# A six-stage decoder megakernel: weights get homes that outlive a stage, and are loaded one stage ahead

## The reference, cut to what matters

```python
x = _layernorm(x + _L0_attn_ref(x, ...))            # state space scan, both directions
x = _layernorm(x + _L0_xattn_ref(ctx_1024, x, ...)) # cross attention, 1500 context rows
x = _layernorm(x + _L0_ffn_ref(x, router_w, w1, w2))  # 8 experts, top 2, squared relu
x = _layernorm(x + _L1_attn_ref(x, ...))            # Mamba block: in_proj, conv, dt, b, c, scan, out_proj
x = _layernorm(x + _L1_xattn_ref(x, ctx_1024, ...)) # causal attention, 16 heads of 8
x = _layernorm(x + _L1_ffn_ref(x, gate_weight, bias, gate_proj, up_proj, down_proj))  # 8 gated experts
```

## Time and profile before

| what | value |
|---|---|
| median of three runs | 1306.85 us |
| the profiled execution, its own time | 1308.4 us |
| its span, first to last instruction | 1306.6 us |
| experts 0, from the stage's first instruction to its last | 728.3 to 807.9 us |
| Mamba: the two loading blocks | 809.1 to 823.7 us |
| Mamba: the scan block | 906.5 to 1115.0 us |
| causal attention, block of the projections | 1134.4 to 1159.3 us |
| experts 1 | 1240.7 to 1306.6 us |

### The profile page before, as it was taken

One profiled execution on the slowest core, in us unless ns is written; L12 is line 12 of the kernel. 1 busy time (PEld: TensorE's weight loads), 2 busy tenths in 40 slices (PEclk: granted clock), 3 DMA queues, 4 the chain that ended last, 5 costly groups with the idle time before them and its releaser, 6 DMA issues. The chain is left out here.

```text
span 1306.6 us, 22904 instructions
## 1 busy us (share of the span) xinstructions
PE 1032.5 (79%) x8295; PEld 737.2 (56%) x8295; DVE 1021.1 (78%) x2092; ACT 699.1 (54%) x1468; POOL 559.6 (43%) x869
## 2 busy tenths in 40 slices
PE   2899887556699999999997793572888888577686
PEld 1555454344699999999996563220333333445555
DVE  4699999666698888899975466549999999567465
ACT  3867554025466666666662442343666666147444
POOL 3100000012888888888853220101777777114351
PEclk9999888768899999999999797665899999879889
DMA  1000000011211111111000100000000000100001
GB/s 42 1 1 2 2 1 1 2 62 47 93 49 72 73 72 72 71 69 69 32 2 1 33 1 19 4 1 0 0 1 1 1 1 1 39 1 3 2 25 29
DMA packets 16850, 32.49 MB, mean 25 GB/s; under 512 B 5073, under 2 KB 11969, under 8 KB 16737
## 3 DMA queue, kind: packets, MB, share of 16 engines
q1 hardware_dynamic: 16736, 31.02, 6.9%
HBM read 30.10 MB, written 0.92 MB: 24 GB/s over the span
## 5 line engine op out<-in xcount | busy, mean ns | idle before, releaser
L1938 POOL TENSOR_TENSOR m_h_in<-m_dtu,m_bs 128x448 f32<-128x448 f32 x128 | 145.0, 1136 | 114.6 <-DVE m_dtu L1971 69.3
L1992 DVE TENSOR_TENSOR_SCAN m_hs<-msp_da,m_h_in 128x448 f32<-128x448 f32 x128 | 138.1, 1079 | 2.9 <-ACT msp_da L1960 1.6
L547 DVE SCALAR_TENSOR_TENSOR l0r_u<-l0r_u,l0r_a_col 128x1024 f32<-128x1024 f32 x110 | 136.1, 1279 | 0.0
L928 POOL TENSOR_TENSOR bl_sc<-bl_sc,bl_topall 125x1456 f32<-125x1456 f32 x32 | 105.3, 3290 | 58.1 <-ACT bl_topall L1090 58.1
L502 ACT ACTIVATE l0r_u<-l0rp_pu 128x512 f32<-128x512 f32 x224 | 111.2, 651 | 33.2 <-PE l0rp_pu L438 33.2
L1910 PE MATMUL msp_py<-m_hc,ident 128*128 128x448 f32 x256 | 119.2, 549 | 0.0
L1951 ACT ACTIVATE m_bs<-msp_pb 128x448 f32<-128x448 f32 x128 | 69.6, 544 | 79.6 <-PE msp_pb L1894 79.4
L438 PE MATMUL l0rp_pu<-l0r_xs,l0r_eb 32*128 32x256 f32 x896 | 101.0, 412 | 4.8 <-ACT l0r_u L502 4.1
L1165 PE MATMUL bl_pS<-b_qw,bl_xcT 128*125 128x112 f32 x768 | 104.0, 278 | 0.0
L641 POOL MEMSET bq_lT<- 128x256 f32 x1 | 0.3, 312 | 236.5 <-POOLq L106 236.5
L1165 PEld LDWEIGHTS bl_pS<-b_qw,bl_xcT 128*125 128x125 f32 x768 | 91.5, 189 | 0.0
(11 more groups left out here) (396 smaller groups left out, 2488.8 us busy)
## 6 DMA issues: line engine op xcount, KB each, us to landing
b_xc<-in_ctx SPq DMA_DIRECT2D x16, 750.0 KB
bl_more<-in_ctx SPq DMA_DIRECT2D x16, 750.0 KB
f_w<-in_L_ffn_w SPq DMA_DIRECT2D x2, 512.0 KB
x_tm<-in_x SPq DMA_DIRECT2D x1, 896.0 KB, 5.9
cl_cT<-in_ctx_headT SPq DMA_DIRECT2D x1, 896.0 KB
out_dram<-x_tm SPq DMA_DIRECT2D x4, 224.0 KB, 2.5
l0s_win<-in_L_attn_in_proj_wT SPq DMA_DIRECT2D x1, 256.0 KB
mi_win<-in_L_attn_in_proj_w SPq DMA_DIRECT2D x1, 256.0 KB
```

The source lines that it names most:

```text
L547: ve.scalar_tensor_tensor(state(c, i, r), prev, a_col[:, :], state(c, i, r), ALU.mult, ALU.add).then_inc(step_done, 1)
L928: pool.tensor_tensor(sc[0:KP, n % 3, :, :], sc[0:KP, n % 3, :, :], over(topall[0:KP, n % 2, :].unsqueeze(1), [KP, KT + 1, QR]), ALU.subtra ...
L1938: pool.tensor_tensor(h_in[:, n % NU, :], dtu[:, half, cols], bs[:, n % NU, :], ALU.mult).then_inc(s["db"], 1)
L1992: ve.tensor_tensor_scan(hs[:, n % NU, :], da[:, n % 2, 0:CH], h_in[:, n % NU, :], 0.0, ALU.mult, ALU.add).then_inc(s["scan"], 1)
```

## The change

Tiles and semaphores of the weights move out of their stages.

- `expert_weights` gives `up` and `down` (4 KB per partition each), both routers and the bias a home from `stage_attention` to the end. `up` and `down` are used by both expert stages in turn.
- `mamba_weights` gives the Mamba block's weights a home from `stage_experts0` to the end of `stage_causal`; `causal_weights` one over `stage_mamba` and `stage_causal`.
- `load_experts0` (5 transfers, both routers and the bias among them) is issued by SP at the head of `stage_context`; `load_mamba` (21) in `stage_experts0`; `load_causal` (8) and `load_experts1` (3) in the scan block of `stage_mamba`.
- The two loading blocks of `stage_mamba` are gone; `wbc` is set to zero by POOL in `stage_experts0`.
- The waits for the loads stay at the first use of the weights, on semaphores that no stage clears. `stage_norm` gets its `ready` argument for the norm `min`, and the projections' block has a wait at the head of PE, DVE and POOL.

```diff
+def load_experts0(core, sp):
+    d = core.dram
+    sp.dma_start(core.route0[:, :], d["L0_ffn_router_wT"]).then_inc(core.loaded0, 16)
+    sp.dma_start(core.route1[:, :], d["L1_ffn_gate_weightT"]).then_inc(core.loaded0, 16)
+    sp.dma_start(core.route_bias[:, :], d["L1_ffn_e_score_correction_bias"].partition_broadcast(T2)).then_inc(core.loaded0, 16)
+    sp.dma_start(core.up[:, :, :], d["L0_ffn_w1"].rearrange("i (e w) -> i e w", e=E)).then_inc(core.loaded0, 16)
+    sp.dma_start(core.down[:, :, :], d["L0_ffn_w2"].rearrange("(e w) o -> w e o", e=E)).then_inc(core.loaded0, 16)
+def load_experts1(core, sp):
+    d, PR = core.dram, E // 2
+    sp.dma_start(core.up[:, 0:PR, :], d["L1_ffn_gate_projT"].rearrange("i (e w) -> i e w", e=PR)).then_inc(core.loaded1, 16)
+    sp.dma_start(core.up[:, PR:E, :], d["L1_ffn_up_projT"].rearrange("i (e w) -> i e w", e=PR)).then_inc(core.loaded1, 16)
+    sp.dma_start(core.down[:, 0:PR, :], d["L1_ffn_down_projT"].rearrange("(e w) o -> w e o", e=PR)).then_inc(core.loaded1, 16)
+def load_mamba(core, sp, zeroed):
...
+        sp.dma_start(dst, src).then_inc(m.loaded, 16)
+    sp.wait_ge(zeroed, 1)
+    for p in range(3):
+        for k, w in enumerate(("b", "c")):
...
+def load_causal(core, sp):
...
+        sp.dma_start(dst, src).then_inc(w.loaded, 16)
@@ stage_context
         @block.sync
         def _(sp):
+            load_experts0(core, sp)
             for n in range(NX0, B):
@@ stage_weighed
             @block.sync
             def _(sp):
-                sp.dma_start(wr[:, :], weights_T).then_inc(s["loads"], 16)
-                load(sp)
+                load_mamba(core, sp, s["zeroed"])
...
                 pool.wait_ge(s["built"], 2)
+                pool.memset(core.mamba.wbc[:, :, :], 0.0).then_inc(s["zeroed"], 1)
                 mixes(pool)
             @block.tensor
             def _(pe):
-                pe.wait_ge(s["loads"], 16)
+                pe.wait_ge(core.loaded0, LOADED0)
@@ stage_experts1
-                pe.wait_ge(s["routing"], 32)
+                pe.wait_ge(core.loaded0, LOADED0)
...
-                pe.wait_ge(s["loads"], 48)
+                pe.wait_ge(core.loaded1, LOADED1)
@@ stage_mamba
-            with nc.Block() as block:
-                @block.vector
-                def _(ve):
-                    ve.memset(wbc[:, :, :], 0.0)
-                @block.sync
-                def _(sp):
...
-                        sp.dma_start(dst, src).then_inc(loads, 16)
-                    sp.wait_ge(loads, 9 * 16)
-            with nc.Block() as block:
-                @block.sync
-                def _(sp):
...
-                    sp.wait_ge(loads, 21 * 16)
-            stage_norm(core, "min", rms=True, residual=False, gain=scale[:, 0:1], outT=by_batch(xnT))
+            stage_norm(core, "min", rms=True, residual=False, gain=scale[:, 0:1], outT=by_batch(xnT),
+                       ready=(core.mamba.loaded, MAMBA_LOADED))
...
+            @block.sync
+            def _(sp):
+                load_causal(core, sp)
+                load_experts1(core, sp)
@@ stage_causal
-                @block.sync
-                def _(sp):
...
-                        sp.dma_start(dst, src).then_inc(loads, 16)
-                    sp.wait_ge(loads, 8 * 16)
...
-                    pe.wait_ge(loads, 8 * 16)
+                    pe.wait_ge(w.loaded, CAUSAL_LOADED)
@@ program
+        expert_weights(core)
         with lent_semaphores(core):
+            stage_attention(core)
+        with ExitStack() as mamba:
+            mamba_weights(core, mamba)
+            with lent_semaphores(core):
+                stage_experts0(core)
+            with ExitStack() as causal:
+                causal_weights(core, causal)
+                with lent_semaphores(core):
+                    stage_mamba(core)
+                with lent_semaphores(core):
+                    stage_causal(core)
```

More of the change, by code:

```diff
@@ L9 @@
 from contextlib import ExitStack, contextmanager
+from dataclasses import dataclass
 import numpy as np
@@ new lines @@
+LOADED0 = 5 * 16
+def load_experts1(core, sp):
[3 more added lines that the diff above has]
+    sp.dma_start(core.down[:, 0:PR, :], d["L1_ffn_down_projT"].rearrange("(e w) o -> w e o", e=PR)).then_inc(core.loaded1, 16)
+LOADED1 = 3 * 16
+@dataclass
+class MambaWeights:
+    col: object
+    alog: object
+    scale: object
+    win: object
+    wdt_in: object
+    wdt_out: object
+    dtb: object
+    wbc: object
+    bcb: object
+    wout: object
+    bout: object
+    loaded: object
@@ new lines, with causal_weights @@
+@dataclass
+class CausalWeights:
+    wqkv: object
+    bqk: object
+    cT: object
+    wp: object
+    bv2: object
+    bp: object
+    loaded: object
+CAUSAL_LOADED = 8 * 16
+def causal_weights(core, ctx):
+    sb, _ = ctx.enter_context(scope(core, "cw"))
+    core.causal = CausalWeights(
+        wqkv=sb("wqkv", [D, 3, D]), bqk=sb("bqk", [D, 2]), cT=sb("cT", [D, T]), wp=sb("wp", [P, D]), bv2=sb("bv2", [P, 2]),
+        bp=sb("bp", [T2, D]), loaded=core.sem("cw_loaded"))
+def load_causal(core, sp):
+    d, w = core.dram, core.causal
+    for dst, src in ((w.wqkv[:, 0, :], d["L1_xattn_Wq"]), (w.wqkv[:, 1:3, :], d["L1_xattn_Wkv"].rearrange("i (k o) -> i k o", k=2)),
+                     (w.bqk[:, :], d["L1_xattn_bqk"]), (w.cT[:, :], d["ctx_headT"]),
+                     (w.wp[:, :], d["L1_xattn_Wp_split"]),
+                     (w.bv2[0:64, :], d["L1_xattn_bv_split"]), (w.bv2[64:P, :], d["L1_xattn_bv_split"]),
+                     (w.bp[:, :], d["L1_xattn_bp"].partition_broadcast(T2))):
+        sp.dma_start(dst, src).then_inc(w.loaded, 16)
@@ L1268, in route, with stage_weighed @@
     chain.base += 5
-def stage_weighed(core, name, weights_T, load, products, openings, mixes, project, expert):
+def stage_weighed(core, name, products, openings, mixes, project, expert):
     nc = core.nc
@@ L1303, in stage_weighed @@
         pj = psum("pj", [P, 2 * HALVES, 512])
-        names = "loads built logits probs projected weighed stats moments roots scales normed".split()
+        names = "zeroed built logits probs projected weighed stats moments roots scales normed".split()
         s = {n: core.sem(f"{name}_{n}") for n in names}
@@ L1517, in stage_experts1 @@
         py = psum("py", [P, NC, 512])
-        names = ("routing loads built logits probs gates ups opened taken mixed cut turned kept wide weighted projected added stats "
+        names = ("built logits probs gates ups opened taken mixed cut turned kept wide weighted projected added stats "
                  "moments roots scales normed written").split()
@@ L1709, in stage_mamba @@
-            with nc.Block() as block:
-                @block.sync
-                def _(sp):
-                    for p in range(3):
-                        for k, w in enumerate(("b", "c")):
-                            at = slice(32 * p + DS * k, 32 * p + DS * (k + 1))
-                            sp.dma_start(wbc[:, :, at], d[f"L1_attn_{w}_proj_w"].rearrange("(h p) s -> p h s", p=P)).then_inc(loads, 16)
-                            sp.dma_start(bcb[at, :], d[f"L1_attn_{w}_proj_b"].rearrange("(p a) -> p a", a=1)).then_inc(loads, 16)
-                    sp.wait_ge(loads, 21 * 16)
@@ L1750, in _ @@
                 def _(pe):
+                    pe.wait_ge(core.mamba.loaded, MAMBA_LOADED)
                     for k in range(2 * H2 * NC):
@@ L2092, in stage_causal @@
             rden = sb2("rden", [P, 2, B // NPR, L])
-            loads, built, pre, zeroed, spread, taken, taken_last = (core.sem(f"cl_{x}") for x in ("loads", "built", "pre", "zeroed", "spread", "taken", "taken_last"))
+            built, pre, zeroed, spread, taken, taken_last = (core.sem(f"cl_{x}") for x in ("built", "pre", "zeroed", "spread", "taken", "taken_last"))
             def pair_at(cg, k):
```

103 lines of the change are left out of this document (47 added, 56 removed).

## The result

The changed kernel's first four runs had a median of 1285.01 us (1284.26 to 1285.78), the kernel before 1307.34 us beside them (1303.47 to 1309.51). The ratio is 0.9831, with a 95% interval of 0.9809 to 0.9853: faster by 1.7%, 22.3 us in the medians. Forecast were 23.1 us and 1283.8 us. The profiled execution took 1284.66 us, its span is 1282.9 us, 23.7 us less than before's.

A forecast was written before the change was run, and what follows sets the result against it. No single engine bounds the kernel (none busy over 79%); stages separated by barriers wait for weight loads at four heads. Gains 1.55 + 14.56 + 3.17 + 3.80 = 23.08 us off the 1306.85 us median give 1283.8 us, range 1279 to 1289.

The forecast's parts named there:

- (a): Head of experts 0: PE's first matmul no longer waits for the router's transfer, whole stage moves; gain 1.55 us.
- (b): Mamba stage's head: both loading blocks with their barriers go, the norm's first statistics start earlier; gain 14.56 us.
- (d): Head of experts 1: PE no longer waits for router and bias, the stage moves as a whole; gain 3.80 us.
- (c): Causal stage's head: DVE, not PE, decides when kblk starts; gain 3.17 us, bounds 1.9 and 7 us.
- The cover of the context tiles: Context block: five transfers ahead of the tiles cost at most 7.1 us against 28 us, so nothing waits; slower case 0.02.
- The 28 us of the prediction: Context block: slack of the first context tile, issued at 324.59 and first used at 352.8.
- The point from which the change would have lost: Context tiles: after 28 + 23 + 4 = 55 us of lateness the kernel is slower than before; chance 0.02.
- The prediction's sign for this cover: Context block: first statistics on bl_more later than 28 us after the block's head would show the cover wrong.
- Contention: Context block: transfers don't slow the engines beside them (POOL's subtraction 3291 against 3290 ns); nothing added.
- Block heads: Rival: a 0.93 us start delay, seen at the causal stage, shows at three heads; 2.8 us, 1286.6 us, chance 0.10.
- the prediction's own sign: Stage heads: the prediction is wrong if any head keeps a wait of over 1 us.
- Clock: PE's restarts: no sign, 2.5 us each way; rivals later clock, about 1289 us, chance 0.07, and earlier, about 1280, 0.04.

The follow-up runs named there:

- e4: Changed kernel with the router's weights, w1 and w2 loaded at the head of experts 0 again: 1284.34 us, ratio 0.9829 to the kernel before.
- e1: Changed kernel with the Mamba block's 21 transfers and DVE's memset of wbc back in two loading blocks at their stage's head: 1293.66 us, again 1294.29 us.
- e3: Changed kernel with the last expert stage's router, bias and three projections loaded at its head again: 1284.81 us, ratio 0.9844 to the kernel before.
- e2: Changed kernel with only the causal stage's 8 transfers back at its head: 1283.23 us, again 1284.79 us.
- e5: Changed kernel with twelve extra PE matmuls between keys and queries in the causal stage: 1285.52 us, ratio 0.9842 to the kernel before.
- e6: Changed kernel with DVE's memset of vblk moved from the causal stage's head to behind the writes of kblk: 1282.29 us, ratio 0.9814 to the kernel before.
- e8: Changed kernel with both expert matrices (1 MB) loaded eight more times ahead of the context tiles: 1306.27 us, ratio 1.0002 to the kernel before.
- f1: e6 with POOL's half of the vblk memset also moved, behind its mask: 1282.73 us, ratio 0.9816 to the kernel before.

## Why the prediction was right, and where its steps were not

**Sizes of the waits: right.** (a), (b) and (d) came out within 0.01, 0.24 and 0.01 us, and e4, e1 and e3 brought the waits back to their places (1.77, 14.7 and 3.3 us). The releasers are those named: the barrier at all three, no transfer.

**What the parts are worth: read from the stages' lengths.** The medians of e2, e3 and e4 don't show their parts, but all fourteen traces together do. Each row is one length in us; "load ahead" has every trace in which that stage's load is ahead and its code is the changed kernel's.

| length | before, two traces | this load back at its stage | load ahead | predicted gain |
|---|---|---|---|---|
| (a) head of experts 0 to its last activation | 79.6, 79.6 | 79.3 (e4) | 76.7 to 77.4 in 11 | 1.55 |
| (b) that activation to the norm's statistics | 15.9, 15.9 | 15.8, 15.8 (e1) | 1.1 in 10 | 14.56 |
| (c) causal head to the last stage's head | 106.3, 102.0 | 106.0, 104.7 (e2) | 100.9 to 102.1 in 7 | 3.17 |
| (d) last stage's head to the end | 65.9, 65.9 | 65.5 (e3) | 62.2 in 11 | 3.80 |

(b) and (d) stand as predicted. (a) was sized too small: it gave 2.2 to 2.9 us, since the stage behind the wait is shorter by another 0.7 to 1.4 us, for which the sum had no term and no experiment shows a cause. That the sum came within a microsecond of the measured 22.3 us is in part luck: in the first pair of traces the 1.3 us more in (a) and the 2.8 us less behind the scores stand against 2.7 us more at the end of and behind the context block and 1.2 us lost with the values.

**(c): right in kind, 0.4 us short at the head, and its worth at the end is not what its head says.** DVE did decide. But its memset began 1.28 us behind the head, 0.35 us more than before, and so `kblk` gained 2.76 us and not 3.17. Of these the block kept 1.5 us in the first pair of traces (25.1 to 23.6), because PE, done early with its keys, idled and then made the values partly at the low clock (granted 0.74, before 1.00). e5 supports that cause: kept busy, PE made the values in 3.79 us and not 5.02. The other traces bear it out: PE's gap ahead of the queries was at most 0.1 us in six, and their values took 3.79 us; 2.5 us in e6, 4.21 us; 3.3 us in e4 and e8, 4.3 us; 3.9 to 4.2 us in the other five, 5.0 to 5.2 us. The other trace of before has a block as short as the changed kernel's (23.6 us) and the same 78.4 us behind it. So by the first trace of before (c) is worth 4.3 us from head to head, by the second nothing; e2's two traces put it at 2.6 to 5.1 us. Nine runs with the load back in place and nine without have the same median. What (c) is worth stays open between nothing and 5 us.

**The cover of the context tiles: right answer, wrong size.** The 28 us of the prediction are the distance from issue to first use. The transfer's own way belongs to it: in e8 the first use came 10.1 us after the issue, with one round's megabyte still on its way in front, as in the changed kernel. The lateness of 41.7 us against the changed kernel cost 24.61 us at DVE, so 17.1 us of slack are left in the changed kernel, the weights already counted. The point from which the change would have lost is not 55 us of lateness: e8 is level with before at 41.7, and 17.1 + 22.3 = 39.4 us follows from its own numbers. The prediction's sign for this cover, first statistics later than 28 us after the block's head, could not tell: it is 28.2 us before and 28.9 in the changed kernel, and DVE waits in neither.

**Contention: none.** From the first to the last statistics on a late tile it is 298.7 or 298.8 us in every trace but e8's, with the megabyte in front or without it.

**Block heads: the rival had one head of four, and less there than it seemed.** The delays at (a), (b) and (d) were 0.04 us or none beyond the barrier. The causal stage's DVE is late by 0.93 us in both traces of before and of e1, and by 1.28 us in all other traces with the large memset first. But 0.80 us of either go with the memset of `vblk`, as e6 and f1 showed. The head's own share is then 0.13 us before (an estimate: 0.93 less 0.80) and 0.47 us in e6 and f1, so the 0.93 us that the rival was built on were mostly not the head's. Why the memset starts late, and why the head's share grew by 0.35 us, the profile doesn't show. By its letter the prediction's own sign, a head that keeps a wait of over 1 us, is met by these 1.28 us, though no load and no semaphore is behind them.

**Clock: right as a range, half wrong as a kind.** I took it for a term without sign that falls independently at each restart. The traces show both. The largest pattern, 4 us in the Mamba projections, was the same in both traces of each kernel that was traced twice: 71.2 and 71.6 us in the two of e1, 75.6 to 76.0 in all others. The one at the scores and the norm behind them is 80.8 to 81.0 us in both of e2, in e5 and in f1, and 78.0 to 78.5 us in the eight other traces with the loads ahead or partly ahead; only the kernel before had one of each (81.2 and 78.4). It goes with the values: the eight had them at over 4 us, five of the six with 3.79 us have the 81. Other stretches changed from execution to execution of one kernel: the end of the context block (50.9 and 49.4 us in the changed one), the stretch between it and experts 0 (26.2 and 24.0 us), and even all that lies ahead of the context block, where nothing differs (323.4 and 325.9 us). Undone one by one, the four parts gave back about 10, 1, 2 and 0 us of the 22 (ratios 0.9914 and 0.9907, 0.9840 and 0.9834, 0.9844, 0.9829 against 0.9831 and 0.9827). For e1 the 14.7 us less the pattern's 4.0 account for it. For the other three the patterns and the scatter of 1.5 to 9 us between executions of one kernel are as large as the part itself, so only the stages' lengths above can tell. Why e1 has its pattern, and the kernel before with the same loading blocks has not, stays open: the projections start at 833.3 and 834.4 in the one and at 836.3 in the other, and no experiment moved that start by itself. If the kernel before had had e1's pattern, the change would have been worth about 18 us.

## What to carry to other kernels

A wait at a stage's head is worth its length only up to the next thing that was waiting in parallel; read who decides the first product behind it, and then check the next two blocks, since a gain that leaves PE idle can come back as clock (1.2 us here), and one that leaves it busy can still be lost behind it (2.6 us in e5 and f1, cause open). Weights can go a stage ahead at no cost where the queue they join has slack; the slack is the distance from issue to first use less the transfer's own time. Parts under 4 us in this kernel of 1300 us are shown by the lengths of their stages, over several traces, and not by medians of a few runs, and undoing parts one by one need not add up.

## What the hardware showed that I had not expected

**The clock falls under a busy PE.** In 7 us with PE busy for 7.00 us the granted clock was 0.57 on the mean in one kernel and 1.00 in another (16 records in 9.90 or 6.28 us). The Trainium skill (TensorE: Matmul & The Clock Gate, Part 1) says that how many matmuls run at the low clock varies from run to run, since the gate's timing doesn't restart with the kernel; the traces agree at the end of the context block (4.43 and 2.90 us for the same 24 records in the two traces of the changed kernel). In the Mamba projections both traces of each kernel that was traced twice agree with each other, and that is what they add.

**POOL's memset shuts out a tiny DVE instruction.** `kbias` (128x4) took 2.86 us beside POOL's memset of 128x4096 and 0.24 us without it. DVE's own memset took 3.47 us beside POOL's memset (3.51 us) and the same 3.47 us without it (e6), and its writes of `kblk` from PSUM took 7.92 us for 12 in f1, beside POOL's memset (3.59 us), and in the changed kernel, where that memset was over. The Trainium skill (SBUF — State Buffer, Who interferes with whom) says that the two engines share one pair of ports as an exclusive lock, which a DVE copy or tensor_scalar can take in a two-port mode, and which an instruction with at most one input from SBUF outside these modes leaves alone. The rows agree, if `kbias` ran in such a mode, which no row says.

**A large memset on DVE starts late.** The memset of 128x4096 has 0.80 us of idle time in front of it in e6 and f1, where it follows another DVE instruction and waits for no semaphore; as the first instruction of its block it came 1.28 us after the head, and a memset of 128x256 in its place 0.47 us. POOL's memset of the same size follows its predecessor at once (1119.12 plus 0.20 us, then 1119.38).
